# A decoder on one Trainium2 core: the last cross-attention as 32 streamed fp32 steps in place of split bf16 operands that pass through DRAM

## The reference

```python
Q = query @ Wq.T + bq; K = key @ Wk.T + bk; V = value @ Wv.T + bv
Q, K, V = (split(Q), split(K), split(V))          # 16 heads of 8
scores = jnp.einsum('bhqd,bhkd->bhqk', Q, K) / jnp.sqrt(jnp.float32(D_K))
scores = jnp.where(mask, -jnp.inf, scores)
attn_w = jax.nn.softmax(scores, axis=-1)
attn_w = jnp.where(jnp.isnan(attn_w), 0.0, attn_w)
out = jnp.einsum('bhqk,bhkd->bhqd', attn_w, V)
return out.transpose(0, 2, 1, 3).reshape(b, -1, D_MODEL) @ Wo.T + bo
```

## Time and profile before

| | |
|---|---|
| median of 3 runs (range) | 1525.31 us (1519.01 to 1525.95) |
| the profiled execution: its time, its span | 1523.25 us, 1521.2 us |
| mean granted TensorE clock in it | 0.927 of full |
| busy over the span: PE, DVE, ACT, POOL | 84%, 47%, 49%, 27% |
| from the first `nx` statistics of the last cross-attention to its last residual | 1213.21 us to 1405.73 us, 192.5 us |
| DMA | 25.55 MB, mean 17 GB/s |

### The profile page before, as it was taken

How to read it: one execution, slowest core, us unless ns; L and a number is a source line. 1 busy time by engine, 2 the same in 40 slices (tenths; PEclk the granted TensorE clock), 3 DMA queues, 4 the chain that set the end, 5 groups by cost and what they waited for, 6 DMA issues and landing times.

```text
span 1521.2 us, 21784 instructions
## 1 busy us (share of the span) xinstructions
PE 1279.8 (84%) x7659; PEld 760.6 (50%) x7666; DVE 716.0 (47%) x2049; ACT 740.8 (49%) x1820; POOL 403.4 (27%) x345
## 2 busy tenths in 40 slices
PE   4599998899998989998989999965997612788688
PEld 2244565454554644555644545544887311333576
DVE  7665644465554455554355564424113561421544
ACT  1276565466666466666547666621443300243332
POOL 0433423443333253332263342211110040000100
PEclk8699999999999999999999999985999855898799
DMA  4000000000000000000000000001110023000010
GB/s 131 0 1 1 22 8 22 12 15 0 22 8 22 8 20 1 22 1 8 22 22 1 1 1 1 1 21 45 29 42 14 0 44 38 3 2 1 9 31 22
DMA packets 29683, 25.55 MB, mean 17 GB/s; under 512 B 4506, under 2 KB 23575, under 8 KB 29591
## 3 DMA queue, kind: packets, MB, share of 16 engines
q1 hardware_dynamic: 29591, 24.33, 6.3%
HBM read 22.71 MB, written 1.61 MB: 16 GB/s over the span
## 4 chain that ended last, share of the span: by engine, by line
PE 76%; DVE 11%; DMA 3%; POOL 3%; issue 3%; ACT 2%; SPq 1%; another core or an unknown queue 0%; DVEq 0%; ACTq 0%; POOLq 0%
PE bank L1487 12%; PE bank L1446 9%; PE bank L1465 8%; PE bank L1506 6%; PE bank L1518 6%; PE bank L1498 4%; PE bank L1695 4%; PE bank L1462 4%; PE bank L1439 3%; PE bank L1511 2%; PE bank L1601 2%; PE bank L1603 2%; PE bank L1602 2%; PE bank L1868 2%; DMA QA<-dram_q 2%
## 5 line engine op out<-in xcount | busy, mean ns | idle before, releaser
L833 DVE CUSTOM_DVE_ANT_0 bank<-bank,maskrow 128x512 f32<-128x512 f32 x256 | 172.4, 716 | 151.5 <-PE bank L1446 151.4
L1215 ACT ACTIVATE probs<-bank,tops 128x512 f32<-128x512 f32 x256 | 174.3, 685 | 128.1 <-DVE tops L833 128.0
L646 POOL TENSOR_TENSOR rot<-rot,sin 128x512 f32<-128x512 f32 (+1 forms) x112 | 134.2, 1199 | 376.3 <-DVE rot L822 376.3
L1227 ACT ACTIVATE KA<-bank 128x512 f32<-128x512 f32 x256 | 139.2, 601 | 31.8 <-PE bank L1465 31.8
L1446 PE MATMUL bank<-QA 64*128 64x512 f32 x512 | 146.7, 653 | 7.6 <-DVE rot L822 7.0
L1465 PEld LDWEIGHTS bank<-ident,probs 128*128 128x128 f32 x1024 | 116.8, 141 | 54.4 <-issue 45.5
L1465 PE MATMUL bank<-ident,probs 128*128 128x128 f32 x1024 | 134.7, 274 | 2.3 <-ACT Vs L1194 2.3
L1487 PE MATMUL bank<-KA,Vs 128*64 128x512 f32 x512 | 135.4, 615 | 0.0
L648 POOL TENSOR_TENSOR QA<-rot 128x512 f32<-128x512 f32 x96 | 121.7, 1268 | 7.5
L1211 ACT ACTIVATE probs<-bank,tops 128x154 f32<-128x154 f32 x256 | 95.5, 383 | 57.2 <-DVE tops L830 56.6
L821 DVE TENSOR_TENSOR rot<-bank,cos 128x512 f32<-128x512 f32 (+1 forms) x112 | 73.9, 660 | 74.3 <-PE bank L1506 55.5
(11 more groups left out here) (252 smaller groups left out, 2288.7 us busy)
## 6 DMA issues: line engine op xcount, KB each, us to landing
f<-in_fW SPq DMA_DIRECT2D x8, 256.0 KB, 3.1
Vc<-in_wup SPq DMA_DIRECT2D x8, 192.0 KB, 2.4
QA<-dram_q SPq DMA_DIRECT2D x6, 256.0 KB
wk<-in_sWk SPq DMA_DIRECT2D x4, 256.0 KB, 2.8
wq<-in_sWq SPq DMA_DIRECT2D x4, 256.0 KB, 3.3
wv<-in_sWv SPq DMA_DIRECT2D x4, 256.0 KB, 4.7
wo<-in_sWo SPq DMA_DIRECT2D x4, 256.0 KB, 2.8
ck<-in_cWk SPq DMA_DIRECT2D x4, 256.0 KB, 2.6
```

Source lines behind the costliest of these rows:

```text
L646: g.tensor_tensor(turned, turned, tab, ALU.mult).then_inc(q.pool_step, 1)
L833: v.tensor_tensor_reduce(bank[i][:, :], bank[i][:, :], maskrow[:, u.b * S:(u.b + 1) * S], -SCALE, 3.0e38, ALU.add, ALU.min, tops[:, g % 4, ...
L1215: c.activation(to, bank[i][:, :], ACT.Exp, bias=tops[:, g % 4, e, 0:1], scale=-1.0, accum_out=sums[:, n, k, e:e + 1]).then_inc(q.probs_rea ...
L1227: c.activation(turned_self(u)[:, half, :, k * P:(k + 1) * P], bank[4 + half][:, :].rearrange("p (c t) -> p c t", t=P), ACT.Copy).then_inc( ...
```

## The change

The scores are now made once, in fp32 and with the queries on the partitions, and nothing of the block goes through DRAM. The block runs in 32 steps (`XSTEPS`). A step takes one tile of 128 queries and four heads (`half` says which two of four 32-row groups of the array, `ii` which two of a group's four heads; `key_rows`, a new constant, zeroes the keys of the other heads in `KZ`, so that one contraction over 32 rows gives a single head's score).

- PE: per step two mask matmuls (bf16, 308 columns), two score matmuls (fp32, 32 rows, 308 columns), and, two steps behind, four turns of 128 keys of the probabilities and one turn of the four heads' last 26 keys, packed to 4 x 32 columns in `xpad`. Eight steps make a unit; its values are multiplied while the next unit runs (`weigh_main`, `weigh_tail`, each four fp32 matmuls into the four 32-column groups of one bank; the tail uses the four 32-row groups as well).
- DVE: two maxima per step, written negated, and a copy of the turned keys (`main_out`). ACT: four exponents per step, with the maximum as bias, and the copies of tails and heads. POOL: one copy into `xpad` per step.
- The turned mask (`maskT`) at the program's start is gone. Keys and values are prepared earlier: `last_keys` stands between statistics and scaling of the norm ahead of the decayed attention, `last_values` in those of the norm after it. POOL's memsets are smaller and move to the first of these norms. The first sequence's statistics for the last norm are taken before the second sequence's residual.

```diff
+        QX = AT[:, 0, :]
+        KZ = ATf[:, NT:NT + 4 * B * C].rearrange("p (b i c) -> p b i c", b=B, i=4)
+        Vx = KA[:, 5120:7168].rearrange("p (i h c) -> p i h c", i=2 * B, h=H1)
+        OX = KA[:, 7168:8192].rearrange("p (b t c) -> p b t c", b=B, t=TB)
+        XP = probs[:, :, :, :].rearrange("p a b c -> p (a b c)")[:, 0:16 * C].rearrange("p (r j c) -> p r j c", r=4, j=4)
+        O4, OXT = [G[:, i, :] for i in range(2)], [G[:, 2 + i, :] for i in range(2)]
...
-            sp.wait_ge(q.parts_ready, 1)
-            sp.dma_start(dram_k[:, :, :].rearrange("a p t -> p a t"), Kb[:, 0:3, 0:B * C]).then_inc(q.parts_out, 16)
-            sp.wait_ge(q.parts_ready, 3)
-            sp.dma_start(dram_q[:, :, :].rearrange("a p t -> p a t"), Qb[:, 0:3, :]).then_inc(q.parts_out, 16)
-            sp.wait_ge(q.parts_out, 32)
-            sp.wait_ge(q.kst_one, 3)
-            for i, (kp, qp) in enumerate(((0, 0), (0, 1), (1, 0), (1, 1), (0, 2), (2, 0))):
-                r = slice(i * DK, (i + 1) * DK)
-                sp.dma_start(Kst[r, :, :], dram_k[kp].rearrange("(h d) t -> d h t", d=DK)).then_inc(q.parts_in, 16)
-                sp.dma_start(Qst[r, :, :], dram_q[qp].rearrange("(h d) t -> d h t", d=DK)).then_inc(q.parts_in, 16)
-            for b in range(B):
-                sp.wait_ge(q.xshT_ready, b + 1)
-                sp.dma_start(dram_s[b], shiftT[:, b, :]).then_inc(q.xsh_out, 16)
-                sp.wait_ge(q.xsh_out, 16 * (b + 1))
-                sp.dma_start(Qst[SPLITS * DK:SPLITS * DK + 2, :, b * S:(b + 1) * S],
-                             dram_s[b].rearrange("(a h) t -> a h t", a=2)).then_inc((q.xsh_in0, q.xsh_in1)[b], 16)
...
+                    g.tensor_copy(xpad[:, hs % 2, :, 0:C2], XP[:, hs % 4, :, P:C]).then_inc(q.xpad_ready, 1)
...
+            g.memset(Vx[:, :, :, DK:32], 0.0).then_inc(q.xpad_zero, 1)
+            g.memset(xpad[:, :, :, :], 0.0).then_inc(q.xpad_zero, 1)
+            pool.wait_ge(q.xpad_zero, 2)
+            g.memset(Vx[:, :, :, DK:DK + 1], 1.0).then_inc(q.xpad_zero, 1)
             norm_powers()
-            g.memset(QA[:, :], 0.0).then_inc(q.kst_one, 1)
-            pool.wait_ge(q.kst_one, 1)
-            g.memset(Kst[DH:P, :, :], 0.0).then_inc(q.kst_one, 1)
-            pool.wait_ge(q.kst_one, 2)
-            g.memset(Kst[0:DH, :, :], 1.0).then_inc(q.kst_one, 1)
+            last_attention()
...
-            def split(dst, src, bias, scale, n):
-                f = SPL[:, 0:n]
-                link(v.tensor_scalar(f, src, bias, scale, ALU.add, ALU.mult))
-                link(v.tensor_copy(dst[0], f))
-                link(v.tensor_tensor(f, f, dst[0], ALU.subtract))
-                link(v.tensor_copy(dst[1], f))
-                return v.tensor_tensor(dst[2], f, dst[1], ALU.subtract)
...
+            def last_keys():
+                dve.wait_ge(q.xk_full, 1)
+                for i in range(4):
+                    ins = v.tensor_scalar(KZ[:, :, i, :], bank[0][:, 0:B * C].rearrange("p (b c) -> p b c", b=B),
+                                          cols[:, 7:8], cols[:, 8 + i:9 + i], ALU.add, ALU.mult)
+                ins.then_inc(q.xk_ready, 1)
+            def last_values():
+                dve.wait_ge(q.xv_full, 1)
+                v.tensor_tensor(Vx[:, :, :, 0:DK], bank[1][:, :].rearrange("p (i h d) -> p i h d", i=2 * B, d=DK),
+                                brow[:, 2, :].rearrange("p (h d) -> p h d", d=DK).unsqueeze(1)
+                                .broadcast_to([P, 2 * B, H1, DK]), ALU.add).then_inc(q.xv_ready, 1)
...
+                def maximum(hs):
+                    n, b, ii, t, half = xstep(hs)
+                    for gg in range(2):
+                        dve.wait_ge(q.xs_full, 2 * hs + gg + 1)
+                        v.tensor_reduce(xtop[:, n, half, t, 2 * gg:2 * gg + 2],
+                                        bank[2 * half + gg][:, 0:2 * C].rearrange("p (a c) -> p a c", a=2),
+                                        AX.X, ALU.max, negate=True).then_inc(q.xm_done, 1)
+                def main_out(hs):
+                    n, b, ii, t, half = xstep(hs)
+                    dve.wait_ge(q.xmain_full, hs + 1)
+                    v.tensor_copy(xmain(n)[:, half, :, t * P:(t + 1) * P],
+                                  bank[4 + hs % 2][:, :].rearrange("p (j q) -> p j q", j=4)).then_inc(q.xmain_out, 1)
...
+                for hs in range(2):
+                    maximum(hs)
+                for hs in range(XSTEPS):
+                    main_out(hs)
+                    if hs + 2 < XSTEPS:
+                        maximum(hs + 2)
+                    if hs >= 8 and hs % 8 == 3:
+                        divide(hs // 8 - 1, 0, bank[7])
+                    if hs >= 8 and hs % 8 == 7:
+                        divide(hs // 8 - 1, 1, bank[7])
+                xresidual(0, bank[2])
+                norm_stats(0, x, False)
+                divide(3, 0, bank[4])
+                divide(3, 1, bank[5])
+                xresidual(1, bank[0])
...
-            norm(x, nx)
+            for b in range(B):
+                norm_stats(b, x, False)
+            last_keys()
+            for b in range(B):
+                norm_scale(b, x, nx, False)
...
+            def last_exps(hs):
+                n, b, ii, t, half = xstep(hs)
+                for j in range(4):
+                    if j % 2 == 0:
+                        act.wait_ge(q.xm_done, 2 * hs + j // 2 + 1)
+                    ins = c.activation(XP[:, hs % 4, j, :], bank[2 * half + j // 2][:, j % 2 * C:(j % 2 + 1) * C], ACT.Exp,
+                                       bias=xtop[:, n, half, t, j:j + 1])
+                ins.then_inc(q.xp_ready, 1)
...
+                c.activation(xtail(n)[:, :, t * P:(t + 1) * P], bank[6][:, 0:2 * P].rearrange("p (h q) -> p h q", h=2),
+                             ACT.Copy).then_inc(q.xtail_out, 1)
...
-            pe.wait_ge(q.mask_ready, see.next(q.mask_ready))
-            for k in range(2):
-                for t in range(TB):
-                    c0 = k * (S // 2) + t * P // 2
-                    ins = turn(bank[3][:, c0:c0 + P // 2].bitcast(BF16), maskq[:, t, k * C2:k * C2 + P], identb[:, :])
-            ins.then_inc(q.maskT_full, 1)
-            lend([3], q.maskT_ready)
...
+            def last_scores(hs):
+                n, b, ii, t, half = xstep(hs)
+                if hs % 16 == 0:
+                    pe.wait_ge(q.xq_ready, b + 1)
+                for gg in range(2):
+                    i = 2 * half + gg
+                    free(i)
+                    mm(bank[i][:, 0:2 * C].rearrange("p (a c) -> p a c", a=2), identb[:, :],
+                       maskq[:, t, :].unsqueeze(1).broadcast_to([P, 2, C]), start=True, stop=False)
+                for gg in range(2):
+                    i = 2 * half + gg
+                    r = slice(32 * i, 32 * i + 32)
+                    mm(bank[i][:, 0:2 * C].rearrange("p (a c) -> p a c", a=2), QX[r, b * S + t * P:b * S + (t + 1) * P],
+                       KZ[r, b, 2 * ii:2 * ii + 2, :], start=False, stop=True).then_inc(q.xs_full, 1)
+                for gg in range(2):
+                    reader[2 * half + gg], read_at[2 * half + gg] = q.xp_ready, hs + 1
+            def last_turns(hs):
+                i = 4 + hs % 2
+                pe.wait_ge(q.xp_ready, hs + 1)
+                free(i)
+                for j in range(4):
+                    ins = turn(bank[i][:, j * P:(j + 1) * P], XP[:, hs % 4, j, 0:P], ident[:, :])
+                ins.then_inc(q.xmain_full, 1)
+                lend([i], q.xmain_out)
+                pe.wait_ge(q.xpad_ready, hs + 1)
+                if hs == 0:
+                    free(6)
+                elif hs % 2 == 0:
+                    pe.wait_ge(q.xtail_out, hs // 2)
+                c0 = hs % 2 * P
+                turn(bank[6][:, c0:c0 + P], xpad[:, hs % 2, :, :].rearrange("p j c -> p (j c)"),
+                     ident[:, :]).then_inc(q.xtail_full, 1)
+            def weigh_main(n, half, i):
+                b, ii = n // 2, n % 2
+                pe.wait_ge(q.xmain_out, 8 * n + 7 + half)
+                if n == 0 and half == 0:
+                    pe.wait_ge(q.xv_ready, 1)
+                free(i)
+                for j in range(4):
+                    mm(bank[i][32 * j:32 * j + 32, :], Vx[:, 2 * b, 4 * (2 * half + j // 2) + 2 * ii + j % 2, :],
+                       xmain(n)[:, half, j, :], start=True, stop=False)
+            def weigh_tail(n, half, i):
+                b, ii = n // 2, n % 2
+                pe.wait_ge(q.xtail_out, 4 * n + 4)
+                for j in range(4):
+                    r = slice(32 * j, 32 * j + 32)
+                    ins = mm(bank[i][r, :], Vx[r, 2 * b + 1, 4 * (2 * half + j // 2) + 2 * ii + j % 2, :],
+                             xtail(n)[r, half, :], start=False, stop=True)
...
+            for hs in range(2):
+                last_scores(hs)
+            for hs in range(XSTEPS):
+                last_turns(hs)
+                if hs + 2 < XSTEPS:
```

(62 more changed lines are left out.)

321 lines of the change are left out of this document (91 added, 230 removed).

## The result

The changed kernel takes 1432.6 us, median of 4 runs (1429.8 to 1434.8), beside 1525.6 for the kernel before on the same chip: a ratio of 0.940, 95% interval 0.938 to 0.942. The forecast was 1447, range 1428 to 1466: inside the range, 14.4 us too slow, and within 0.5 us of the rival *four groups abreast*, 1433. The profiled execution took 1429.8 us with a span of 1427.9.

A forecast was written before the change was run, and what follows sets the result against it. Waits, not an engine, were taken to bound the last cross-attention. 77.6 + 1.4 + 2.1 - 2.6 = 78.5 us less than the profiled 1523.3 gave 1444.8; with 2.1 for the median, 1447, range 1428 to 1466.

The forecast's parts named there:

- four groups abreast: Rival for the `weigh` matmuls: four column groups run beside each other, 0.98 us per `weigh`, kernel 1433 us; chance 0.27.
- What bounds the kernel: Last cross-attention, 192.6 us: no engine bounds it; waits include scalings beside POOL's fill (12.5 us) and query read-back (30.9).
- Way in and one pass: Block start: first statistics to first scores, 10.6 us, then first step's masks to its first turn at low clock, 3.7.
- First eight steps: First eight of the block's 32 steps, without `weigh`: two steps take 3.55 us, eight take 14.2.
- The other 24: Remaining 24 steps, PE running without waiting: 2.69 us a step with each `weigh` at 1.84, 62.6 us in all.
- Way out: Block end: gather, four `weigh` and first output, 11.8 us; then statistics, divisions and second output at low clock, 12.1.
- Around it: Outside the block: last norm 1.4 us less, program start 2.1 less, ahead of the decayed attention 2.6 more.
- pairs abreast: Main case for the `weigh` matmuls: two column groups run beside each other, 1.84 us per `weigh`, kernel 1447 us; chance 0.45.
- The tails one after another: Rival for `weigh_tail`: its four matmuls, writing one bank, run singly, 3.5 us instead of 1.84, kernel 1460 us; chance 0.18.
- PE at half clock: Rival for the whole block: PE's clock stays at its lower level, 86 us more, kernel 1533 us; chance 0.03.
- The hand-overs bind: Rival for the 32 steps: PE waits each step for exponents or DVE's order, 0.4 us a step, kernel 1460; chance 0.07.

The follow-up runs named there:

- e3_fill_back: Changed kernel with one of the three removed POOL fills put back after the opening norm's reciprocal roots: 1439.2 us (ratio 0.944).
- e5_before_no_dram: Kernel before the change without the last cross-attention's 18 DRAM transfers, PE waiting for POOL's fills instead: 1478.1 us (ratio 0.970).
- e1_two_groups: Changed kernel with the four matmuls of each `weigh_main` writing two column groups instead of four, tails unchanged: 1439.8 us (ratio 0.945).
- e7_way_out: Changed kernel with its way out reordered and the output bias as one 512-column matmul instead of four of 128: 1424.7 us (ratio 0.935).
- e10_pairs: Changed kernel with `weigh_main` and `weigh_tail` merged in pairs, two mains then their two tails, twice: 1447.9 us (ratio 0.950).
- e4_scores_twice: Changed kernel with the mask and score matmuls of all 32 steps issued a second time: 1466.0 us (ratio 0.961).
- e2_interleaved: Changed kernel with `weigh_main` and `weigh_tail` merged and issued head by head, main then tail: 1480.0 us (ratio 0.971).
- e1_one_group: Changed kernel with all four matmuls of each `weigh_main` writing one column group instead of four, tails unchanged: 1452.0 us (ratio 0.953).

## Why the prediction was right, and its one wrong price

*What bounds the kernel.* Right: the scalings beside the fill (`e3_fill_back`) and the read-back (`e5_before_no_dram`) were waits. Their removal gave, by the marks in the profiles, 10.4 and 49.3 us.

*Way in and one pass*, 10.6 + 3.7: measured 9.4 + 3.0. The two projections took 2.77 us against 3.59 in the earlier trace rows, at a higher clock (0.86 over this stretch, where the kernel before waited out the fills). The first pass did not run at low clock, as I had it: from 1223.66 to 1226.66 the granted clock is 1.00, so the 0.8 that I added for it was not there.

*First eight steps*, 14.2: measured 14.3 (1226.66 to 1240.93). The form, a pass of 2.9 us shared by two steps, holds: from a step's first mask to its turns are 2.97 us (1227.26 to 1230.23). Two of its terms were off and nearly cancel, the two masks at 0.36 us instead of 0.26 and the five turns at 0.60 instead of 0.66.

*The other 24*, 62.6: measured 52.9. This is the term that was mis-sized, by its item "A `weigh` is four fp32 matmuls ... I take 1.84". It took 0.99 to 1.00. Twelve of the 16 fall here and make 10.2 us; 9.7 were missed. I had taken the price of the nearest row, which has two column groups, over the mechanism that I had named as a rival: twice as many groups, half the time. `e1_two_groups` brings the 1.84 back for the mains.

*Way out*, 11.8 + 12.1: measured 7.9 (1293.85 to 1301.7) + 12.3. Four `weigh` are 3.4 of the 3.9 missed. The sum of the second half was right by luck in part: the divisions took 0.8 and 0.9 us instead of 1.0 each, the gather at low clock 1.16 instead of 0.7. `e7_way_out` shows that much of this half was a matter of order.

*Around it.* The last norm: scaling starts 1.4 us after the last statistics begin, 1.4 less, as forecast. Ahead of the decayed attention PE's turns come 6.27 us after the statistics, 2.3 more than before; forecast 2.6. At the start I expected 2.1 us less and got 1.2: PE's first turns of `nx` are at 12.58, not by 11.7. Without the mask's turn PE waits for the context, which came in later than in the profile before:

```profile
12.04 0.75 PE L1592 MATMUL bank<-ident,probs 77*128 77x77 f32 x4 [12.04 <-DMA probs<-in_ctx]
12.58 1.92 PE L1383 MATMUL bank<-ident,nx 128*128 128x128 f32 x8
```

This is no accident of one profile. In all eleven traces of the changed kernel and its variants the context's first matmul starts between 12.04 and 13.15, in the two of the kernel before (10.74, and 10.62 without transfers) earlier. Why it lands later is open.

*The sum.* The profiled executions differ by 93.5 us, forecast 78.5. Of the 15.0 between them the 16 `weigh` are 13.6. So the step of my sum that failed is the price of a `weigh`, 1.84 us where four column groups abreast took 0.99 to 1.00. The range held because it took in both bounds of this price; the case that I gave the largest chance, pairs abreast, is not what happened.

*The rivals.* "Four groups abreast" is what happened, for mains and tails. "The tails one after another" did not: four tails with row groups and column groups of their own write one bank within 0.99 us (and two of them within 0.98 in `e10_pairs`). The rule cited for it, from the Trainium skill, TensorEngine Tiling (Array Packing), section Restrictions and Gotchas, is not borne out for these tiles, which lie on the diagonal of the array; no run here has two row groups write the same partitions. "PE at half clock" did not either: the granted clock is 1.00 through all steps, a third of which are turns. The Trainium skill, TensorE: Matmul & The Clock Gate, section Part 4: PE-mode transpose, has turns not count as activity the same way; here they cost no clock as long as PE did not idle. "The hand-overs bind" did not in the 24 full steps: PE is busy in 52.8 of 52.9 us, and `e4_scores_twice` is slower by PE's own extra work.

## What to carry to other kernels

Where the nearest row has two of something side by side and the new code has four, price the mechanism too, and let row and mechanism be the two bounds. Group small matmuls by the form of their tile: the same eight took 2.0, 3.9 or 7.8 us by their order alone. Near the end of a block look for side work that stands ahead of the last link of the chain; moving it, together with one bias matmul in place of four, was worth 8 us.

## What the hardware showed that I had not expected

- Column groups took their matmuls whatever the order of issue between them: first, first, second, second lasted 1.85 us, as first, second in turn (1.84).
- Between a tile of 128 rows and one of 32 rows nothing overlapped, even in different column groups, and each change cost about 0.1 us beside it, an estimate (0.97 for a matmul in `e2_interleaved` that takes 3.55/4 = 0.89 behind its like in `e1_one_group`).
- A POOL fill of 6.9 us held DVE's scalings to its end (`e3_fill_back`), while DVE's own fill of 1.76 us ran inside another POOL fill of 4.23 us (the kernel before).
